# Self attention and its projection in float32r halves held in SBUF, two heads per pass of the array

## The chip, the cores and the metric

The kernel runs on one core of one Trainium2 chip. The metric is the device time of one execution in microseconds (us); of several executions the median is given. Engines are named PE (TensorE matmul), PEld (its weight loads), DVE (VectorE), ACT (ScalarE), POOL (GpSimd) and SP (SyncE, which only begins DMAs here).

## What is computed

Two decoder layers on x of 2 x 1024 tokens by 256. The change touches only the first sublayer, and the way the constants, the tokens and the context matrix reach SBUF ahead of it:

```python
def _L0_attn_ref(x, Wqkv, bqkv, Wout, bout):          # 16 heads of 16
    qkv = jnp.einsum('bsd,hde->bhse', x, Wqkv) + bqkv[None, :, None, :]
    q, k, v = jnp.split(qkv, 3, axis=-1)
    score = jnp.einsum('bhsd,bhtd->bhst', q, k)
    score = jnp.where(causal[None, None], score, -jnp.inf)
    attn = jax.nn.softmax(score / jnp.sqrt(16), axis=-1)
    y = jnp.einsum('bhst,bhtd->bhsd', attn, v)
    return y.transpose(0, 2, 1, 3).reshape(b, s, d) @ Wout + bout
...
x = x + _L0_attn_ref(_layernorm(x), ...)
```

After it come cross attention, a feed-forward part, a recurrence, a second cross attention and a mixture of experts, which the diff leaves alone.

## The kernel before

The program is a row of blocks; at the end of each, all engines meet.

`setup` (L111) loads the tokens and lets POOL make identity and masks; `make_context` (L802) transposes the context. `project_self` (L242) normalises the tokens (`LayerNorm`), transposes them, and forms q and k in float32 (16 sums of two float32 matmuls of 512 tokens, L306; the profile has two records for each float32 matmul), then v (L316). ACT and DVE cut every q and k into three bfloat16 parts (L334 to L366), and SP writes them to DRAM (L276). 32 DMAs (L268) bring the biases for q and k, one for each head.

`SelfAttention(Attention)` (L693, L413) works in 8 units: one batch entry and four heads each. SP brings a unit's q and k from DRAM into a slot (L740, 12 DMAs of 128 KB), three units ahead, laid out so that 96 rows of one matmul hold the six products of parts. Each unit has two phases. In the first, a *piece* is one score matmul of 128 queries by up to 512 keys (L751); where the block lies on the diagonal a mask is added by a second matmul (L754), and DVE takes the row maxima from PSUM (L759). Pieces alternate between two PSUM banks. The maxima are transposed (*turn*, L538), negated, cut into three parts by DVE (L636 to L649) and sent by SP (L504) as three more rows under q. In the second phase a *chunk* (L772, mask L776) gives the scores transposed with the maximum already taken off, ACT takes the exponential (L787), and *weigh* (L796) multiplies four heads' weights by v into one PSUM area, each head in its own 32 columns of the array. ACT copies the sum out (L586), PE transposes it (L568) and DVE divides (L662, L666).

PE carries out all of this in one fixed order, which `order` writes out: unit u's chunks are mixed evenly with unit u + 1's pieces. Every engine is in order, so a wait of PE holds all that stands behind it. The first unit's pieces have no chunks beside them; the last unit's chunks have no pieces.

`project_out` (L830) is the same before and after.

Of the kernel before, what the change touches and what calls it, by code (L numbers as in the profile page):

```python
# [110 lines left out]
def setup(c):  # L111

    nc = c.nc
    x_in, const, cast = c.sig("x_in"), c.sig("const"), c.sig("const_cast")
    with nc.Block() as block:
        @block.sync
        def _(sp):
            for b in range(4):
                sp.dma_start(c.x[:, 4 * b:4 * b + 4, :],
                                      c.arg["x"].rearrange("b (t p) d -> p (b t) d", p=P)[:, 4 * b:4 * b + 4, :]).then_inc(x_in.sem, 16)  # L120
            sp.wait_ge(x_in.sem, x_in.at(64))

        @block.gpsimd
        def _(pool):
            link = Chain(const)
            pool.memset(c.ident[:, :], 0.0).then_inc(link.sem, 1)
            pool.wait_ge(link.sem, link.next())
            pool.affine_select(out=c.ident[:, :], in_=c.ident[:, :], compare_op=ALU.not_equal, fill=1.0,
                                    base=0, pattern=[[-1, P]], channel_multiplier=1).then_inc(link.sem, 1)
            pool.wait_ge(link.sem, link.next())  # L130
            pool.memset(c.maxmask[:, :], 0.0).then_inc(link.sem, 1)
            pool.wait_ge(link.sem, link.next())

            pool.affine_select(out=c.maxmask[:, :], in_=c.maxmask[:, :], compare_op=ALU.is_ge, fill=MASKED,
                                    base=0, pattern=[[-1, P]], channel_multiplier=1).then_inc(link.sem, 1)
            pool.wait_ge(link.sem, link.next())
            pool.memset(c.expmask[:, :], 0.0).then_inc(link.sem, 1)
            pool.wait_ge(link.sem, link.next())

            pool.affine_select(out=c.expmask[:, :], in_=c.expmask[:, :], compare_op=ALU.is_ge, fill=MASKED,  # L140
                                    base=0, pattern=[[1, P]], channel_multiplier=-1).then_inc(link.sem, 1)
            pool.wait_ge(link.sem, link.next())
            pool.iota(c.iota[:, :], [[1, 8]], base=0, channel_multiplier=0,
                           allow_small_or_imprecise_dtypes=True).then_inc(link.sem, 1)
            pool.wait_ge(link.sem, link.next())

        @block.vector
        def _(dve):
            dve.wait_ge(const.sem, const.at(2))
            dve.tensor_copy(c.identb[:, :], c.ident[:, :]).then_inc(cast.sem, 1)  # L150
    for signal, n in ((x_in, 64), (const, 7), (cast, 1)):
        signal.passed(n)


# [78 lines left out]
def head_parts(c, ctx, name):  # L233

    t = {}
    t["full"] = c.sb(ctx, name + "_full", [P, 2, 512], F32)
    t["rest"] = c.sb(ctx, name + "_rest", [P, 2, 512], F32)
    t["part"] = c.sb(ctx, name + "_part", [P, 2, PARTS, N], BF16)
    return t


def project_self(c, v_all, scr_q, scr_k):  # L242

    nc, ps = c.nc, c.ps
    wqkv, bqkv = c.arg["L0_attn_Wqkv"], c.arg["L0_attn_bqkv"]
    with ExitStack() as ctx:
        ln = LayerNorm(c, ctx, "ln0")
        xt = c.sb(ctx, "xt0", [P, KD, N], F32)
        w = c.sb(ctx, "w_qkv", [P, KD, H, 3 * DH], F32)
        w_qk = c.sb(ctx, "w_qk", [P, 2, KD, D], F32)  # L250
        bias = c.sb(ctx, "b_qk", [P, 2, KD], F32)
        bias_v = c.sb(ctx, "b_v", [P, H, DH], F32)
        t = head_parts(c, ctx, "h0")
        w_in, full, high, rest, mid, low, sent, v_set, v_zero = (
            c.sig("w_in"), c.sig("pr_full"), c.sig("pr_high"), c.sig("pr_rest"), c.sig("pr_mid"), c.sig("pr_low"),
            c.sig("pr_sent"), c.sig("pr_v"), c.sig("pr_vzero"))
        mm = c.sig("pr_mm")
        w_set = c.sig("pr_wset")
        blocks = [(i, mb) for i in range(2) for mb in range(KD)]
        NC = N // 512  # L260
        with nc.Block() as block:
            @block.sync
            def _(sp):
                for k in range(KD):
                    sp.dma_start(w[:, k, :, :], wqkv.rearrange("h (k p) e -> k p h e", p=P)[k]).then_inc(w_in.sem, 16)
                for i in range(2):
                    for h in range(H):
                        sp.dma_start(bias[DH * (h % 8):DH * (h % 8) + DH, i, h // 8:h // 8 + 1],  # L268
                                              bqkv[h:h + 1, DH * i:DH * i + DH].rearrange("a b -> b a")).then_inc(w_in.sem, 16)
                sp.dma_start(bias_v[:, :, :], bqkv[:, 2 * DH:3 * DH].partition_broadcast(P)).then_inc(w_in.sem, 16)  # L270
                for n, (i, mb) in enumerate(blocks):

                    sp.wait_ge(mid.sem, mid.at(NC * (n + 1)))
# [75 lines left out]
            def _(dve):  # L349
# [9 lines left out]
                for n in range(len(blocks) * NC):  # L359
# [8 lines left out]
                    if n >= 1:  # L368
                        lows(n - 1)
# [3047 lines left out]
```

## Time and profile before

| what | us |
|---|---|
| median of 3 runs (1902.81 to 1908.55) | 1905.12 |
| the profiled execution | 1912.87 |
| its span, first to last instruction | 1911.2 |
| front blocks, to the last value of v | 0 to 84 |
| memory fills and first loads of the attention, no matmul | 84 to 112 |
| first unit's pieces alone, to its turn | 112 to 144 |
| seven units' pieces beside the chunks of the unit before | 144 to 414.5 |
| the last chunks, no pieces | 414.5 to 455.5 |
| the output projection of the attention | 455.5 to 480.5 |
| all the rest | 480.5 to 1911 |

A busy time counts an instruction from its start to its end; matmuls overlap in the array, so the distance between the starts of two of them tells what one takes in a stream, while the duration of one holds the way through the array as well. [...]

### The profile page before, as it was taken

How to read it: one execution, taken by the hardware profiler on the slowest of the kernel's cores; microseconds unless marked ns; L12 is line 12 of the kernel's file. 1: busy time of each engine (PE TensorE's matmuls, PEld its weight loads, DVE VectorE, ACT ScalarE, POOL GpSimd, SP SyncE). 2: the span in 40 equal slices, each digit the busy share in tenths (PEclk: the TensorE clock that was granted, in tenths of full speed). 3: DMA queues.
4: the chain of work that ended last, by engine and by line, in shares of the span. 5: the costliest groups of instructions: out<-in, count | busy, mean ns of one | idle time of the engine just before them, and what ended most of it. 6: DMA issues, size and time to landing. Idle time of an engine off the chain costs nothing. (4 is left out here: it accounts for less than half of the span.)

```text
span 1911.2 us, 28538 instructions
## 1 busy us (share of the span) xinstructions
PE 1438.0 (75%) x10307; PEld 1073.4 (56%) x10307; DVE 1089.6 (57%) x2450; ACT 898.0 (47%) x2137; POOL 308.2 (16%) x338
## 2 busy tenths in 40 slices
PE   4758889988589999789981453588868059999964
PEld 2413333334379999656760231477755059999953
DVE  3657766741655555455668647456553047777753
ACT  1503555553256666331104775366542057887731
POOL 1200000002223333200001525100010600000034
PEclk8858999998799999979995665799887579999987
DMA  2371322200200000110000000211112256766623
GB/s 68 132 99 20 49 35 35 35 2 9 81 1 2 1 1 2 34 39 1 0 23 9 1 6 14 64 35 34 34 47 88 88 188 219 222 216 217 227 85 103
DMA packets 92688, 122.59 MB, mean 64 GB/s; under 512 B 22221, under 2 KB 74051, under 8 KB 92291
## 3 DMA queue, kind: packets, MB, share of 16 engines
q1 hardware_dynamic: 86675, 105.85, 20.5%
q0 software_dynamic: 4912, 14.42, 2.1%
q8 instruction: 83, 1.36, 0.3%
q10 hardware_dynamic: 960, 0.47, 0.1%
q14 instruction: 58, 0.48, 0.1%
HBM read 88.60 MB, written 24.67 MB: 59 GB/s over the span
## 5 line engine op out<-in xcount | busy, mean ns | idle before, releaser
L759 DVE TENSOR_REDUCE sa_top<-ps 128x1 f32<-128x512 f32 (+3 forms) x384 | 197.2, 553 | 96.3 <-PE ps L751 65.3
L787 ACT ACTIVATE sa_probs<-ps 128x1024 f32<-128x1024 f32 (+4 forms) x192 | 150.8, 811 | 204.1 <-PE ps L772 145.6
L751 PE MATMUL ps<-sa_k,sa_q 96*128 96x512 bf16 (+3 forms) x384 | 125.5, 365 | 55.5 <-DMA sa_k<-scr_k 28.5
L1983 PE MATMUL ps<-me_h,me_w_parts 128*128 128x256 f32 x1104 | 142.0, 289 | 14.5 <-DVE me_w_parts L2058 7.9
L1983 PEld LDWEIGHTS ps<-me_h,me_w_parts 128*128 128x128 f32 x1104 | 136.8, 192 | 18.7 <-issue 15.3
L1997 PE MATMUL ps<-me_w_parts,me_mid 128*128 128x256 f32 x1104 | 136.2, 283 | 6.1 <-DVE me_result L2075 6.1
L1997 PEld LDWEIGHTS ps<-me_w_parts,me_mid 128*128 128x128 f32 x1104 | 132.3, 188 | 10.5 <-issue 10.5
L2735 ACT ACTIVATE cx_p<-ps,cx_top 128x154 f32<-128x154 f32 x256 | 97.2, 389 | 86.4 <-DVE cx_top L2799 86.4
L751 PEld LDWEIGHTS ps<-sa_k,sa_q 96*128 96x128 bf16 x384 | 35.1, 98 | 160.7 <-DVE sa_top L759 89.1
L2058 DVE TENSOR_TENSOR me_w_parts<-me_chunk,me_w_parts 128x1024 fp32r<-128x1024 f32 x92 | 112.8, 1226 | 21.4 <-ACT me_w_parts L2023 18.6
L2045 ACT ACTIVATE me_full<-ps,me_b 128x256 f32<-128x256 f32 x184 | 95.0, 517 | 57.6 <-PE ps L1983 54.5
L2086 DVE TENSOR_TENSOR me_mid<-me_full,me_mid 128x256 fp32r<-128x256 f32 x184 | 76.9, 422 | 65.8 <-ACT me_mid L2047 65.8
L772 PE MATMUL ps<-sa_q,sa_k 99*128 99x512 bf16 (+3 forms) x384 | 108.2, 335 | 7.6 <-ACT sa_probs L787 7.5
L2023 ACT ACTIVATE me_w_parts<-me_chunk 128x1024 fp32r<-128x1024 f32 x92 | 104.6, 1137 | 3.8 <-DMA me_chunk<-in_L_ffn_W_dram 3.8
L3164 ACT ACTIVATE cn_p<-ps,cn_top 128x154 f32<-128x154 f32 x256 | 82.1, 397 | 43.7 <-DVE cn_top L3248 43.5
L2047 ACT ACTIVATE me_mid<-ps,me_b 128x256 fp32r<-128x256 f32 x184 | 96.2, 523 | 0.0
L2597 POOL TENSOR_TENSOR cx_pn<-cx_p,cx_rinv 128x512 f32<-128x512 f32 x64 | 66.8, 1043 | 171.3 <-DVE cx_rinv L2807 171.2
L1058 PE MATMUL ps<-f_w_high,f_hid 128*128 128x512 f32 (+1 forms) x320 | 91.9, 373 | 0.0
L796 PE MATMUL ps<-sa_probs,v_all 128*32 128x512 f32 (+3 forms) x768 | 76.9, 503 | 0.0
L850 POOL TENSOR_TENSOR x<-x,po_b 128x256 f32<-128x256 f32 x16 | 11.0, 727 | 361.8 <-DMA po_w<-in_L_attn_Wout_dram 361.8
L772 PEld LDWEIGHTS ps<-sa_q,sa_k 99*128 99x128 bf16 x384 | 38.0, 100 | 49.5 <-ACT sa_probs L787 16.9
L1957 POOL DMA_DIRECT2D moe_results<-me_result x23 | 16.6, 720 | 301.1 <-DVE me_result L2075 301.1
(397 smaller groups left out, 3530.7 us busy)
## 6 DMA issues: line engine op xcount, KB each, us to landing
me_chunk<-in_L_ffn_W_dram SPq DMA_DIRECT2D x92, 512.0 KB, 5.4
sa_q<-scr_q SPq DMA_DIRECT2D x48, 128.0 KB, 4.8
sa_k<-scr_k SPq DMA_DIRECT2D x48, 128.0 KB, 7.7
moe_rows<-mp_zeros SPq DMA_DIRECT2D x2, 2944.0 KB, 12.7
me_row<-moe_rows SPq DMA_DIRECT2D x23, 256.0 KB, 3.8
moe_results<-me_result POOLq DMA_DIRECT2D x23, 256.0 KB, 3.2
cn_qd<-cn_qh SPq DMA_DIRECT2D x64, 64.0 KB, 2.0
scr_q<-h_part SPq DMA_DIRECT2D x6, 512.0 KB, 3.9
```

Of the source, the lines that this page charges most:

```text
L751: last = pe.matmul(c.ps[:, bank, 0:w], self.q_st[0:96, slot, h, P * sb:P * sb + P], self.k_st[0:96, slot, h, k0:k0 + w], start=True, stop= ...
L759: return dve.tensor_reduce(self.top2[:, k0 // 512, ST * h + sb:ST * h + sb + 1], self.c.ps[:, bank, 0:w], AX.X, ALU.max)
L772: last = pe.matmul(out[:, 0:qw], self.k_st[0:KROWS, slot, h, P * kb:P * kb + P], self.q_st[0:KROWS, slot, h, P * kb + q0:P * kb + q0 + qw] ...
L787: return act.activation(dst, src, ACT.Exp, scale=self.width ** -0.5)
L1058: last = pe.matmul(ps[:, 4 + n % 4, 0:w], hid[:, g % 2, net, m, part, cols], wt[:, m, w0:w0 + w], start=(i == 0), stop=(i == len(terms) - 1))
L1983: last = pe.matmul(ps[:, MID + n % 4, 0:RT], w[:, u % 2, 0, i, DM * k + P * b:DM * k + P * b + P], h[:, u % 2, j, k, :], start=(m == 0), s ...
L1997: last = pe.matmul(ps[:, OUT + n % 2, 0:D], mid[:, u % 2, b, i, P * a:P * a + P], w[:, u % 2, 1, j, D * b:D * b + D], start=(m == 0), stop ...
L2023: act.activation(part(n, 0), chunk[:, n % BUF, :], ACT.Copy).then_inc(w_high.sem, 1)
L2045: act.activation(full[:, n % 4, :], ps[:, MID + n % 4, 0:RT], ACT.Relu, bias=col).then_inc(s_full.sem, 1)
L2047: act.activation(mid[:, u % 2, b, 0, :], ps[:, MID + n % 4, 0:RT], ACT.Relu, bias=col).then_inc(high.sem, 1)
L2058: dve.tensor_tensor(part(n, 1), chunk[:, n % BUF, :], raw(part(n, 0)), ALU.subtract).then_inc(w_low.sem, 1)
L2735: last = act.activation(p[:, h + i, :], ps[:, S_BANK + n % SR, M * i:M * i + M], ACT.Exp, bias=top[:, t % 2, h + i:h + i + 1], accum_out=d ...
```

## The change

`setup`, `make_context` and `project_self` become one block, `front`. Tokens come in four DMAs with a semaphore each, in between other loads. The biases go through a small DRAM tensor and come back in four DMAs. ACT does the scaling of the LayerNorm. Tokens and weights are cut into two float32r halves (high and low), and each product of the projection is three float32r matmuls (high by high, high by low, low by high) in place of one in float32: per group of 512 tokens 4 blocks x 6 matmuls of 512 columns and 4 x 6 of 256. q and k stay in SBUF as two float32r halves (`hi`, `lo`); nothing is written to DRAM. POOL cuts the weights (6 copies, 6 subtractions).

`SelfAttention` is rewritten. A head's scores need 3 x 16 = 48 rows, at rows 0 to 47 for one head and 64 to 111 for another, so that two matmuls (`for a in range(2)`) use different halves of the array. Units are halved into 16 subs by queries (`SUBS`): the lower half of the queries has 8 piece pairs and 8 chunk pairs, the upper half 16 and 16. The number and width of DVE's reductions is unchanged (384), as is that of the exponentials' elements. SP alone begins all copies from `hi` and `lo` to the slots, 24 of 64 KB for each unit. Pieces, turns and outs share a ring of three PSUM banks; a pair waits for both its banks at once. `order` sorts by a timetable in which a sub's chunks begin 5 us after its maxima and then follow one another at ACT's pace. POOL fills 32 rows of two halves of the key tile with ones, 6144 float32 columns each, and SP waits for that. The maxima take two parts in place of three.

```diff
 class SelfAttention:
+    SLOTS = 3
+    MAX_RING = 3
+    EXP_BANK = (3, 5)
+    OUT_BANK = 7
...
+        self.k = sb("k", [P, self.SLOTS, 2, S], F32R)
...
+        for k in range(len(SUBS)):
+            for n, (p, sb, k0, w) in enumerate(self.pieces(k)):
+                items.append((dve, "piece", k, n))
+                dve += 2 * (0.075 + w / 960)
+            items.append((dve, "join", k, 0))
+            items.append((dve + 1.2, "turn", k, 0))
+            dve += 1.0
+            act = max(act, dve + 5.0)
+            for n, (kb, p) in enumerate(self.chunks(k)):
+                items.append((act - 0.9, "chunk", k, n))
+                act += 0.12 + 2 * self.span(k, kb)[1] / 1200
+                if p == 1:
+                    items.append((act + 0.9, "weigh", k, kb))
+            items.append((act + 1.0, "copy", k, 0))
+            items.append((act + 3.0, "out", k, 0))
+            act += 0.6
+            dve += 0.9
...
+        def stage(eng, u, i, dst, done):
+            b, g = UNITS[u]
+            for a in range(2):
+                for j, part in enumerate(((self.hi, self.lo, self.hi), (self.hi, self.hi, self.lo))[i]):
+                    for p in range(2):
+                        r = 64 * (g % 2) + 32 * p + DH * a
+                        to = raw(dst[64 * a + DH * j:64 * a + DH * j + DH, u % self.SLOTS])
+                        src = raw(part[r:r + DH, KD * i + g // 2, S * b:S * b + S])
...
+            def _(sp):
+                for u in range(min(self.SLOTS, len(UNITS))):
+                    if u == 0:
+                        sp.wait_ge(s["made"].sem, s["made"].at(2))
+                    stage(sp, u, 0, self.q, self.q_in[u])
+                    stage(sp, u, 1, self.k, self.k_in[u])
+                for k, (u, half) in enumerate(SUBS):
+                    sp.wait_ge(s["freed"].sem, s["freed"].at(uses["turn", k, 0][0] + 1))
+                    for part, neg in enumerate((self.negh, self.negl)):
+                        for a in range(2):
...
+                    if k % 2 and k >= 3 and (k - 3) // 2 + self.SLOTS < len(UNITS):
+                        v = (k - 3) // 2
+                        sp.wait_ge(s["weighed"].sem, s["weighed"].at(step0[last_of_unit[v] + 1]))
+                        stage(sp, v + self.SLOTS, 0, self.q, self.q_in[v % self.SLOTS])
+                        stage(sp, v + self.SLOTS, 1, self.k, self.k_in[v % self.SLOTS])
...
+            def _(pool):
+                for a in range(2):
+                    pool.memset(self.k[64 * a + 32:64 * a + 64, :, :, :].bitcast(F32), 1.0).then_inc(s["made"].sem, 1)
...
+                    banks = [take(m) for m in uses["piece", k, n]]
...
+                    for a in range(2):
+                        r = slice(64 * a, 64 * a + 3 * DH)
+                        last = pe.matmul(ps[:, banks[a], 0:w], self.q[r, slot, half, p, q0:q0 + P], self.k[r, slot, p, k0:k0 + w],
+                                         start=True, stop=not diagonal)
...
+                    if diagonal:
+                        for a in range(2):
+                            pe.matmul(ps[:, banks[a], w - P:w], c.identb[:, :], c.maxmask[:, :], start=False,
+                                      stop=True).then_inc(s["filled"].sem, 1)
```

## Rows read from the trace of the kernel before

**Rows 1.** Busy time by stretch: stretch, us, then PE, PEld, DVE, ACT, POOL, clock, DMA share, GB/s.

```profile
0.00:84.10 84.10, 54.66 (x168) 32.38 (x168) 43.52 (x110) 31.87 (x57) 7.31 (x17) 0.94 0.35 114
84.10:111.80 27.70, 0.00 (x0) 0.00 (x0) 7.00 (x2) 1.28 (x1) 13.86 (x4) 0.53 0.50 67
111.80:144.40 32.60, 24.81 (x80) 6.77 (x80) 25.35 (x49) 0.00 (x0) 0.00 (x0) 0.50 0.68 89
144.40:414.60 270.20, 242.09 (x1785) 102.16 (x1789) 190.39 (x404) 134.70 (x168) 0.00 (x0) 0.97 0.22 31
414.60:455.50 40.90, 32.47 (x260) 12.44 (x255) 3.54 (x12) 23.53 (x33) 0.00 (x0) 0.92 0.01 2
```

**Rows 2.** The page's costliest groups (line, form, count; busy us, mean ns; idle before, releaser).

```profile
L759 DVE TENSOR_REDUCE sa_top<-ps 128x1 f32<-128x512 f32 (+3 forms) x384 | 197.2, 553 | 96.3 <-PE ps L751 65.3
L787 ACT ACTIVATE sa_probs<-ps 128x1024 f32<-128x1024 f32 (+4 forms) x192 | 150.8, 811 | 204.1 <-PE ps L772 145.6
```

**Rows 3.** Timeline up to the first piece (start us, duration us, engine and instruction, idle before).

```profile
15.21 1.41 DVE L175 BATCH_NORM_STATS2 ln_stats<-x 128x6 f32<-128x256 f32 x4 [0.32 <-PEq L808]
...
32.97 0.42 SPq L270 DMA_DIRECT2D b_v<-in_L_attn_bqkv_dram  x1
...
38.52 30.72 PE L306 MATMUL ps<-xt,w_qk 128*128 128x512 f32 x64 [7.99 <-POOL w_qk L289]
...
43.77 0.34 PEld L306 LDWEIGHTS ps<-xt,w_qk 128*128 128x128 f32 x1 [0.52 <-issue]
...
44.61 0.19 PEld L306 LDWEIGHTS ps<-xt,w_qk 128*128 128x128 f32 x1 [0.50 <-issue]
...
84.11 13.86 POOL L726 MEMSET sa_k<- 32x4096 bf16 x4 [45.69 <-POOLq L261]
...
98.00 2.67 SPq L740 DMA_DIRECT2D sa_q<-scr_q  x6
...
111.85 1.03 PE L751 MATMUL ps<-sa_k,sa_q 96*128 96x512 bf16 x2 [28.49 <-DMA sa_k<-scr_k]
```

**Rows 4.** Groups by form, ACT, DVE and POOL: durations used for `front` and the fills.

```profile
L1328 ACT ACTIVATE bi_y<-bi_y,bi_shift,bi_scale 128x256 f32<-128x256 f32 x48 | 25.3, 608 | 22.6 <-DVE bi_minus L1320 22.6
...
L366 DVE TENSOR_TENSOR h_rest<-h_full,h_part 128x512 f32<-128x512 f32 x16 | 11.1, 693 | 23.6 <-ACT h_part L336 23.6
...
L282 POOL MEMSET v_all<- 128x4096 f32 x1 | 3.5, 3512 | 12.0 <-POOLq L808 12.0
```

**Rows 5.** Timeline of PE in the first cross attention: float32r matmuls of 256 columns.

```profile
600.90 0.28 PE L2681 MATMUL ps<-cx_woh,cx_ol 128*128 128x256 f32 x1
601.02 0.28 PE L2681 MATMUL ps<-cx_wol,cx_oh 128*128 128x256 f32 x1
```

**Rows 6.** Issue time on SP of 64 KB and 128 KB copies (duration ns min/median/max).

```profile
L2972 SPq DMA_DIRECT2D cn_qd<-cn_qh x64: 585/597/1601, 1208.9 to 1377.6; - x64
...
L740 SPq DMA_DIRECT2D sa_q<-scr_q x48: 330/426/583, 98.0 to 342.4; - x48
```

**Rows 7.** The page's DMA issues (KB each, median us to landing): an SBUF to SBUF copy.

```profile
cn_qd<-cn_qh SPq DMA_DIRECT2D x64, 64.0 KB, 2.0
```

**Rows 8.** Timeline of PE around one *weigh*, clock 1.00.

```profile
380.01 0.27 PE L772 MATMUL ps<-sa_q,sa_k 99*128 99x256 bf16 x1
380.12 0.22 PE L776 MATMUL ps<-expmask,identb 128*128 128x128 bf16 x1
380.27 1.06 PE L796 MATMUL ps<-sa_probs,v_all 128*32 128x512 f32 x8
381.27 0.61 PE L751 MATMUL ps<-sa_k,sa_q 96*128 96x512 bf16 x2
```

**Rows 9.** Groups by form: DVE's steps for each unit, and ACT's widest exponential.

```profile
L636 DVE TENSOR_SCALAR sa_neg_rest<-ps 32x128 f32<-32x128 f32 x8 | 2.2, 278 | 3.7 <-PE ps L538 3.7
L666 DVE TENSOR_TENSOR o_tok<-ps,sa_rinv 128x256 f32<-128x256 f32 x16 | 6.8, 424 | 0.6
L787 ACT ACTIVATE sa_probs<-ps 128x1024 f32<-128x1024 f32 x48 | 46.9, 1023 | 89.0 <-PE ps L772 72.6 <-PE ps L796 13.0 <-PE ps L776 3.4
```

More of the change, by code:

```diff
@@ L108, in new_stage @@
         self.signals = {}
[L111 to L152, printed above, removed]
 class LayerNorm:
@@ L230, in done, with front @@
             self.s[k].passed(n)
[L233 to L242, printed above, removed]
+VC = DH + 1
+def front(c, ct, hi, lo, v_all, scratch):
     nc, ps = c.nc, c.ps
     wqkv, bqkv = c.arg["L0_attn_Wqkv"], c.arg["L0_attn_bqkv"]
+    scr_b = scratch("scr_b0", [3, H, DH], F32)
+    G = NT // 4
@@ L246, in project_self @@
     with ExitStack() as ctx:
[L247 to L260, printed above, removed]
+        sb = lambda n, shape, dt=F32: c.sb(ctx, "fr_" + n, shape, dt)
+        raw_ctx = sb("ctx", [MH, 4, DC])
+        w = sb("w", [P, KD, H, 3 * DH])
+        wh, wl = sb("wh", [P, 3, KD, D], F32R), sb("wl", [P, 3, KD, D], F32R)
+        bias, bias_v = sb("b", [P, 2, KD]), sb("bv", [P, H, DH])
+        stats, mv = sb("stats", [P, NT, 6]), sb("mv", [P, NT, 2])
@@ L261, in project_self @@
+        c_turned, c_set, turned, x_high, x_low, filled, high, cleared = (
+            c.sig("f_" + k) for k in ("c_turned", "c_set", "turned", "x_high", "x_low", "filled", "high", "cleared"))
+        NB = 5
+        T_BANK, R_BANK, RING = 0, 4, 4
+        blocks = [(i, m) for i in range(2) for m in range(KD)]
+        PER = len(blocks) + 4
         with nc.Block() as block:
@@ L266, in _ @@
+                sp.dma_start(raw_ctx[:, :, :], c.arg["ctx_768"].rearrange("b (i m) d -> m (b i) d", m=MH)).then_inc(c_in.sem, 16)
+                sp.wait_ge(b_out.sem, b_out.at(16))
                 for i in range(2):
[L267 to L270, printed above, removed]
@@ L271, in _ @@
[L271 to L278 removed]
+                    for m in range(KD):
+                        sp.dma_start(bias[:, i, m:m + 1],
+                                     scr_b[i, 8 * m:8 * m + 8, :].rearrange("h (e a) -> (h e) a", a=1)).then_inc(b_in.sem, 16)
@@ L310, in _ @@
-                for u in range(NT):
-                    if u < 8:
-                        pe.wait_ge(high.sem, high.at(n - 7 + u))
-                    else:
-                        pe.wait_ge(v_set.sem, v_set.at(u - 7))
-                    for k in range(KD):
-                        last = pe.matmul(ps[:, (n + u) % 8, 0:D], xt[:, k, P * u:P * u + P],
-                                         w[:, k, :, 2 * DH:3 * DH], start=(k == 0), stop=(k == KD - 1))
-                    last.then_inc(mm.sem, 1)
```

841 lines of the change are left out of this document (395 added, 446 removed).

## The prediction

> **What bounds the kernel now.** I read the page's costliest groups first, then the busy time by stretch, then the timeline at the borders of the stretches. The change ends where the output projection of the attention begins, at 455.5 us of the span; the 1455.7 us behind that run the same instructions on the same data layout and are taken as unchanged. The sum is made against the profiled execution, 1912.87 us, which lies 7.75 us above the median of the runs shown (1905.12); the difference that I find is taken off the median at the end. A difference under 0.3% (5.7 us) can hardly be told from none here.
>
> The 455.5 us fall in two. Up to the first piece of the attention, at 111.85 us [rows 3], the array is often idle: it works 54.7 of the first 84 us and not at all in the next 27.7 [rows 1]. The projection's first matmul comes at 38.52, since POOL copies the weights only after the last of 35 loads (the one for v's bias is begun at 32.97), and between the projection's end and the first piece stand POOL's fills, 13.86 us, and the loads of the first unit, begun at 98.0 and waited for until 111.85 [rows 3]. From the first piece on, 343.6 us, no engine is full by itself: the first unit's pieces take 32.6 us, then seven units take 270.2, that is 38.6 each, and the last chunks 40.9 [rows 1]. In the middle stretch PE is busy 242.1 of 270.2 us, DVE 190.4, ACT 134.7 [rows 1]. DVE's reductions are the largest group, 197.2 us, and stand idle 96.3 us, most of it for pieces [rows 2]. So PE, in its fixed order, sets the pace, and DVE would be next with 220.1 us: 197.2 [rows 2] and 16 times the small steps of a sub, two like the negation at 0.28, the division at 0.42 [rows 9], and join and reciprocal, which I put at 0.45 together by the same rows: 1.43 x 16 = 22.9.
>
> **Up to the first piece.** The first tokens are begun at the start, as now; I allow 4.8 us for them. Then: statistics 1.41 for four tiles [rows 3] and 0.5 for the small steps after them, about 0.7 for root, reciprocal and shift, four normalisations on ACT at 0.61 [rows 4] (2.4), eight transposes 2.3, the high half about 1.2, the low half 0.7 like the subtraction of 693 ns [rows 4]: 14.0, with the semaphores 14.5 us. The weights are begun before 4 us and cut by about 17 us, and the first product needs a third of that; the biases come in six DMAs instead of 33. Both are hidden by the LayerNorm; if they were 3 us late, all that follows is 3 us late. PE's part is then 4 groups of 24 matmuls of 512 and 24 of 256 columns. A float32r matmul of 256 columns takes 0.12 us in a stream [rows 5]; with 0.23 for 512 that is 8.4 us for each group, 33.6 in all, plus 4.6 for the two transpose groups that stand between them. The clock is low at first: loads came 0.85 us apart until 44.6 and half that afterwards, six us after the first matmul [rows 3]; 3 us for that. DVE has 16 low halves at 0.69, and ACT as many high ones, less than PE in each group. The end is 14.5 + 33.6 + 4.6 + 3.0 + 0.8 for the last values = 56.5 us, against 84.1.
>
> What comes after is not shorter by much. A fill of 4096 elements takes 3.51 us in float32 and 3.47 in bfloat16 (13.86 / 4) [rows 3, 4], so it goes by elements; the new ones have 6144, 5.27 us each, 10.5 for both, and SP waits for both: 67.4. Then 24 copies of 64 KB instead of 12 of 128 KB. Issue takes 0.60 for a copy from SBUF to SBUF and 0.43 for a plain one from DRAM [rows 6]; the copies of q have the form of the former and those of k that of the latter, so I take 0.55, with 0.43 and 0.65 as ends. 24 x 0.55 = 13.2, and 2.0 to land [rows 7]: the first piece at 82.6 instead of 111.85, **29.2 us gained**. The DRAM copies of the parts that fall away lay under PE's v matmuls and give nothing by themselves.
>
> **The SP queue.** Now the maxima's rows go out when they are ready. After the change SP begins three whole units before it looks at the first sub: 72 x 0.55 = 39.6 us, then four row copies at 0.6 (2.4) and 1.9 to land, so the first rows arrive 43.9 us after the first copy was begun, 28.7 after the first piece. PE comes to the first chunk after about 12 us (6.5 for the first sub's reductions, 1.0, and 5 less 0.9 by the timetable). Everything that stands behind it on PE, pieces too, waits 16.7 us; DVE can still empty the ring: **16 lost**. Later SP loads a unit after each of the subs 3, 5, 7, 9 and 11, 13.2 us, and the next sub's rows stand behind it. They arrive 2.4 + 13.2 + 2.4 + 1.9 = 19.9 us after the turn before. After subs 3, 7 and 11 comes a short sub (some 11 us) and PE wants them after 15: 4.9 late, of which DVE hides 1.5: **10 lost** in three places (none if PE is late itself, 15 at most).
>
> **The piece and chunk work.** ACT's exponentials come in bursts. A two-head exponential of 1024 elements takes 0.98 in a stream (46.9 / 48) [rows 9]; an upper sub has 16, eight of them narrower, 13.6 us; a lower one 5.5. In 13.6 us DVE wants 12 pairs of pieces (24 pairs in 27.5 us), in 5.5 about 5. What PE needs for this:
> - [...] I take 0.24 for every width.
> - A diagonal pair has two masks more, each 0.055 (from L776 to L772, 0.06 [rows 8]): 0.11. They use all 128 rows, so the array changes between half height and full height and back.
> - A weigh: 0.85 of columns; entering it costs 0.10 (the mask before it started 0.15 earlier and needs 0.055) and leaving it 0.15 (1.00 from start to start) [rows 8]. Wide 1.10, the narrower ones 0.78 on average.
>
> No row has a change of height. Its bounds are 0, as between L772 and L776, which follow each other without a gap, and 0.10 to 0.15, as around the weigh [rows 8]. Nearest is the weigh, another change of how the array is cut; but there four heads' loads must come first as well, so I take **0.05**. Counting the written order, there are 461 such changes and 178 around weighs.
>
> [...]
>
> Upper burst: 8 x 0.24 + 8 x (0.24 + 0.11 + 0.10) + 4 x 1.10 + 4 x 0.78 + 12 piece pairs, one third plain and two thirds diagonal, at 0.38 (4.6) = 17.6 us against 13.6; lower: 8 x 0.45 + 4 x 0.78 + 5 x 0.38 = 8.6 against 5.5. So PE is late by 4.0 + 3.1, say 7.3 with the transposes, in each of seven units: **51 us** on top of DVE's 220. Between bursts PE has pieces only, and before the change that was done at a clock of 0.50 (112 to 144 us) [rows 1]; the timetable has four gaps of near 10 us. Each costs up to 3 us until the clock is back, as in the projection; PE's lateness shortens them: **8 us** (0 to 30). After the last maxima there remain the end of sub 14's exponentials and sub 15's: **20 us**, against 40.9 now.
>
> Sum from the first piece: 220 + 16 + 10 + 51 + 8 + 20 = 325 us against 343.6, **18.6 gained**. Together with 29.2 it is 47.8: the profiled execution would take 1865, the median 1905.1 - 47.8 = **1857 us**.
>
> **The rivals.**
> 1. *The change of height is free*, or PE's order leaves slack enough. Then a diagonal pair takes 0.35, the bursts are late by 2.4 and 2.1, 32 us in all: 1838. With no lateness of PE at all it is 1806. For it speaks that masks follow without any gap now [rows 8]; against it, that the present unit takes 38.6 us where PE's streams sum to about 31, so that in-order waiting costs something always.
> 2. *It is as dear as around the weigh*, 0.10 to 0.15: 70 to 90 us late instead of 51, 1876 to 1896.
> 3. *The two heads don't run side by side*, since the change doesn't do what it says. Then a pair of 512 columns takes 0.45; 84 us late, 1890. No row has two matmuls in different rows; that the weigh runs four heads in the time of one (0.85 for what would be 3.4) [rows 8] speaks against it for columns. [...]
> 4. *Slower: one after another and dear changes together.* PE's upper burst then takes 24.9 against 13.6 and the lower 12.2 against 5.5: 18 us a unit, 126 in all, and 4 more in the tail. That is 404 from the first piece: 1936. It decides as soon as PE is late by 14 us a unit.
> 5. *Slower: SP falls behind.* Should a copy hold SP for 1.0 us (the worst of the present ones took 1.6 [rows 6]), the first unit lands 10.8 later, the first stall grows by 21, and after each load the next rows are 16 us late after short subs and 3.5 after long ones: 54 instead of 10. 76 us more: 1933. It decides from 0.8 us a copy. The median of 0.60 and the landing in 2.0 [rows 6, 7] speak against it.
>
> **How the numbers follow.** My forecast (1843 to 1872) has 0.48; rival 1, 0.22; rival 2, 0.12; rival 3, 0.05; rival 4, 0.06; rival 5, 0.07. Faster by over 0.3% means under 1899.4: the forecast, rival 1, 0.10 of rival 2 and 0.01 of rival 3: 0.81. Within 0.3%: 0.02 and 0.04 of rivals 2 and 3: 0.06. Slower: rivals 4 and 5: 0.13. The range reaches from rival 1 without lateness, 1805, to just past rivals 2 and 3, 1910, and leaves out rivals 4 and 5 and the little below 1805.
>
> **What would show it.** The first matmul of `front`'s products near 14 us and the fills from 56 to 67; the first piece near 83; then a stall of PE of some 16 us at the first chunk, waiting for a DMA. Two matmuls of a pair starting within 0.1 us of each other; the distance from the second to the mask, less 0.21, is the price of the change of height. Reductions must still be busy 197 us, idle much less than 96. If ACT's idle time in bursts is small and DVE is busy over nine tenths, rival 1 holds; if pairs start 0.21 apart, rival 3. The prediction fails if the clock stays at 0.50 beyond the first unit, which I price at 30 us at most.

## The result, and the profile after

The changed kernel is slower: 1988.96 us median of 4 runs (1979.21 to 1995.48) beside 1904.49 for the kernel before (1902.81 to 1908.55), a ratio of 1.0436 with a 95% interval of 1.0384 to 1.0488. The profiled execution has a span of 1993.5 us, 82.3 more than before.

Busy time by stretch (columns as in [rows 1]): the front end, the gap before the first piece, the first pieces and chunks, the middle up to the last piece, the last chunks.

```profile
0.00:61.50 61.50, 43.41 (x232) 36.97 (x232) 32.06 (x86) 25.18 (x45) 8.84 (x24) 0.97 0.23 54
61.50:89.40 27.90, 0.00 (x1) 0.03 (x1) 0.00 (x1) 1.28 (x1) 10.42 (x2) 0.58 0.35 58
89.40:133.00 43.60, 21.31 (x89) 9.20 (x89) 15.48 (x35) 4.26 (x5) 0.00 (x0) 0.50 0.43 71
133.00:520.80 387.80, 345.75 (x1877) 135.20 (x1873) 200.61 (x423) 140.93 (x181) 0.00 (x0) 0.64 0.13 22
520.80:545.00 24.20, 20.07 (x169) 7.89 (x167) 1.92 (x6) 15.55 (x22) 0.00 (x0) 0.98 0.01 3
```

The first piece comes at 89.4 in place of 111.85, 22.4 us earlier [rows 3]. The part behind the attention takes 1450 us in place of 1456. All of the loss lies between: from the first piece to the last output of the attention (at 543.3, before 455.2) it is 453.9 us in place of 343.4. PE is again the busiest, 345.75 of 387.80 us in the middle, but the granted clock there is 0.64 where it was 0.97 [rows 1]. Every record of the granted clock in this trace is 1.00 or 0.50, 32 of each, so 0.64 means that the array stood at 0.50 for some seven tenths of the stretch.

The page's groups, to be held against [rows 2]: the reductions and the exponentials are as long as before, and their idle time is what grew, for DVE from 96.3 to 215.5 us.

```profile
L675 DVE TENSOR_REDUCE sa_top<-ps 128x1 f32<-128x512 f32 (+3 forms) x384 | 196.2, 553 | 215.5 <-PE ps L592 145.5
L653 ACT ACTIVATE sa_probs<-ps 128x1024 f32<-128x1024 f32 (+1 forms) x192 | 152.4, 810 | 298.0 <-PE ps L617 173.8
L586 PE MATMUL ps<-sa_k,sa_q 48*128 48x512 f32 (+3 forms) x384 | 114.6, 586 | 69.9 <-DVE sa_top L675 40.8
```

Timeline of the changed kernel at the start of the attention: the fills, the first copies, the first pair, and the wait at the first chunk.

```profile
61.79 10.47 POOL L565 MEMSET sa_k<- 32x6144 f32 x2 [46.30 <-POOLq L220]
...
72.29 1.32 SPq L535 DMA_DIRECT2D sa_q<-qk_high  x2
73.66 1.23 SPq L535 DMA_DIRECT2D sa_q<-qk_low  x2
74.93 2.50 SPq L535 DMA_DIRECT2D sa_q<-qk_high  x4
...
89.40 0.47 PE L586 MATMUL ps<-sa_k,sa_q 48*128 48x128 f32 x2 [28.36 <-DMA sa_k<-qk_low]
...
122.58 0.80 PE L613 MATMUL ps<-sa_q,sa_k 50*128 50x512 f32 x2 [14.62 <-DMA sa_q<-sa_negl]
```

And two places in PE's timeline at full clock, 1.00. A pair stands in one line ("x2"); both heads start within 0.04 us of each other.

```profile
454.61 0.50 PE L586 MATMUL ps<-sa_k,sa_q 48*128 48x512 f32 x2
454.94 0.33 PE L613 MATMUL ps<-sa_q,sa_k 50*128 50x384 f32 x2
...
524.28 0.50 PE L613 MATMUL ps<-sa_q,sa_k 50*128 50x512 f32 x2
524.71 0.29 PE L617 MATMUL ps<-expmask,identb 128*128 128x128 bf16 x2
524.93 0.50 PE L613 MATMUL ps<-sa_q,sa_k 50*128 50x512 f32 x2
```

So the heads do run side by side: a pair of 512 columns is followed by the next pair 0.33 us later, where one after another would need 0.43 for the columns alone: at full clock a matmul of 512 columns is followed by the next 0.21 us later (e5, at 282.63). 0.33 is 0.21 for the columns and 0.12 more. A float32r weight load that is not hidden would fit, as an estimate of mine (the loads of these pairs last 0.18 us each from 440 to 460, those of the bfloat16 masks 0.10, and float32r matmuls of 256 columns stood 0.12 apart [rows 5]); no run tests it. With masks it is 0.43 from the pair to them and 0.22 from them to the next pair: 0.10 more going in, and 0.11 more than the masks' own columns (0.107 at that rate) going out. A diagonal pair of 512 columns costs 0.65 where the prediction had 0.45 for every width.

The clock is not low everywhere in this kernel. From 440 to 460 us, with pieces and chunks, and in the last chunks from 520.8 us on, it is 1.00 and 0.98, with the same pairs of 48 and 50 rows a head.

### The profile page after: what moved, and what is told of

Same layout as the page of the kernel before. It is cut to its first block and busy times, and to the rows that moved or that the text cites. A ratio compares the mean times of both kernels' runs of the same rounds, so it can differ in the third digit from the quotient of the medians.

```text
span 1993.5 us, 28893 instructions
## 1 busy us (share of the span) xinstructions
PE 1522.3 (76%) x10379; PEld 1112.4 (56%) x10379; DVE 1069.6 (54%) x2424; ACT 892.9 (45%) x2133; POOL 305.8 (15%) x343
## 5 line engine op out<-in xcount | busy, mean ns | idle before, releaser
L675 DVE TENSOR_REDUCE sa_top<-ps 128x1 f32<-128x512 f32 (+3 forms) x384 | 196.2, 553 | 215.5 <-PE ps L592 145.5
L653 ACT ACTIVATE sa_probs<-ps 128x1024 f32<-128x1024 f32 (+1 forms) x192 | 152.4, 810 | 298.0 <-PE ps L617 173.8
L586 PE MATMUL ps<-sa_k,sa_q 48*128 48x512 f32 (+3 forms) x384 | 114.6, 586 | 69.9 <-DVE sa_top L675 40.8
L1908 PEld LDWEIGHTS ps<-me_w_parts,me_mid 128*128 128x128 f32 x1104 | 132.6, 188 | 10.5 <-issue 10.5
L586 PEld LDWEIGHTS ps<-sa_k,sa_q 48*128 48x128 f32 x384 | 52.6, 254 | 132.6 <-DVE sa_top L675 83.3
L613 PE MATMUL ps<-sa_q,sa_k 50*128 50x512 f32 (+3 forms) x384 | 106.8, 560 | 15.8 <-DMA sa_q<-sa_negl 14.6
L628 PE MATMUL ps<-sa_probs,v_all 128*17 128x512 f32 (+3 forms) x768 | 112.2, 674 | 0.0
L613 PEld LDWEIGHTS ps<-sa_q,sa_k 50*128 50x128 f32 x384 | 48.5, 251 | 97.5 <-issue 51.3
L969 PEld LDWEIGHTS ps<-f_w_high,f_hid 128*128 128x128 f32 x320 | 58.2, 189 | 11.7 <-issue 1.4
```

Source lines behind the costliest of these rows:

```text
L586: last = pe.matmul(ps[:, banks[a], 0:w], self.q[r, slot, half, p, q0:q0 + P], self.k[r, slot, p, k0:k0 + w], start=True, stop=not diagonal)
L613: last = pe.matmul(ps[:, bank + a, 0:w], self.k[r, slot, p, P * kb:P * kb + P], self.q[r, slot, half, p, q0:q0 + w], start=True, stop=not ...
L628: last = pe.matmul(ps[VW * h:VW * h + VC, self.OUT_BANK, q0:HALF], self.v_all[:, ST * b + kb, HPU * g + h, :], self.probs[:, (step0[k] + k ...
L653: act.activation(self.probs[:, (g // 2) % self.PROBS, p, :, 0:w], ps[:, bank:bank + 2, 0:w], ACT.Exp, scale=DH ** -0.5).then_inc(s["exped" ...
L675: dve.tensor_reduce(self.top2[:, k % 2, k0 // 512, col:col + 1], ps[:, m % self.MAX_RING, 0:w], AX.X, ALU.max).then_inc(s["freed"].sem, 1)
L969: last = pe.matmul(ps[:, 4 + n % 4, 0:w], hid[:, g % 2, net, m, part, cols], wt[:, m, w0:w0 + w], start=(i == 0), stop=(i == len(terms) - 1))
```

## The experiments

Two causes stood open. Theory C: the granted clock is the loss, and short bursts with gaps between them keep it low. Theory S: the changes of height are the loss. The second experiment brought theory R: the clock is the loss, and it follows the rows that the matmuls use. Differences of a few us between kernels that were not timed side by side are not read; "attention" is the stretch from the first piece to the last output in the profiled execution.

| kernel | ratio to before (95%) | median us | attention us | clock in it |
|---|---|---|---|---|
| before | 1 | 1904.5 | 343 | 0.92 |
| changed | 1.0436 (1.0384 to 1.0488) | 1989.0 | 454 | 0.65 |
| e1 masks at half height | 1.0196 (1.0141 to 1.0252) | 1947.1 | 406 | 0.67 |
| e2 one after another | 1.1348 (1.1326 to 1.1370) | 2165.6 | 623 | 0.51 |
| e3 chunks twice | 1.0342 (1.0316 to 1.0367) | 1971.8 | 432 | 0.78 |
| e4 chunks spread | 1.0375 (1.0349 to 1.0401) | 1976.4 | 431 | 0.68 |
| e5 before, 48 rows | 1.0435 (1.0399 to 1.0471) | 1988.4 | 428 | 0.65 |
| e6 full height, zeros | 1.0308 (1.0274 to 1.0342) | 1962.1 | 424 | 0.82 |
| e7 e6, masks 64 rows | 1.0529 (1.0482 to 1.0576) | 2006.3 | 465 | 0.79 |
| e8 e6, no maxima's masks | 1.0165 (1.0137 to 1.0192) | 1937.6 | 403 | 0.82 |
| e9 before, 66 rows | 1.0174 (1.0112 to 1.0236) | 1935.4 | 380 | 0.79 |
| e10 before, no maxima's masks | 0.9962 (0.9943 to 0.9982) | 1894.4 | 335 | 0.93 |
| e11 combined | 0.9888 (0.9857 to 0.9920) | 1881.2 | 353 | 0.88 |
| e12 e11, later copies | 0.9905 (0.9881 to 0.9929) | 1878.2 | 359 | 0.87 |

**e1: masks at half height.**

```diff
-  pe.matmul(ps[:, banks[a], w - P:w], c.identb[:, :], c.maxmask[:, :], start=False,
+  r = slice(64 * a, 64 * a + 64)
+  pe.matmul(ps[:, banks[a], w - P:w], c.identb[r, :], c.maxmask[r, :], start=False,
```

(and the same for expmask)

> The changed kernel with each mask matmul on the same 64 rows as the head whose scores it masks (rows 0 to 63 for the first head, 64 to 127 for the second), so that no mask changes the height of the rows used. Left out: the other half of each mask, so half of the masked scores are counted. It takes away 256 of the 461 changes of height in the attention, and keeps every column. Theory S (the changes of height are the loss: 0.22 us in and 0.11 out at full clock, 0.30 and 0.11 at half, with the gaps that follow): 80 to 110 us less than the changed kernel, 1880 to 1910. Theory C (the granted clock is the loss: 0.64 in the attention where the kernel before had 0.97, because two heads beside each other leave the array with gaps between short bursts): the clock stays below 0.75 in the attention and the time is 1945 to 1975.

42 us less than the changed kernel, with the clock still at 0.67. The time, 1947, lies at the lower edge of what theory C allowed and far from the 1880 to 1910 of theory S. Yet the attention is 48 us shorter, so the changes beside the masks are a real part of the loss, less than half of the 110 us. Counted in the written order, all changes of height fall from 569 to 217, so 352 are gone, not the 256 of the expectation (256 is the number of groups of masks). The masks also use fewer rows here, which the run does not keep apart.

**e2: one after another.**

```diff
-  r = slice(64 * a, 64 * a + 3 * DH)
+  r = slice(0, 3 * DH)
```

> The changed kernel with both heads of a pair read from rows 0 to 47 (0 to 49 in the chunks), so that the two matmuls run one after another. Left out: the odd heads' own queries and keys (the even head's stand in their place). Instructions, waits and changes of height stay as they are; the columns that TensorE streams for scores double. Theory C: the array is in use for longer without a gap, the granted clock goes to 0.9 or more in the attention, and the time is 1900 to 1990, no slower than the changed kernel. Theory S: the clock has no part in it, the pairs' doubled columns add 0.21 us at full clock to each 512-column pair and 0.4 at half, and the time is 2030 to 2080.

Busy time of e2 from the first piece to the last output:

```profile
90.40:713.50 623.10, 576.77 (x2128) 265.40 (x2128) 218.67 (x464) 163.37 (x208) 0.00 (x0) 0.51 0.11 19
```

It is 177 us slower than the changed kernel, and both theories miss it, C most of all: PE is busy for 0.93 of the time and the clock is at its lower level almost throughout. Idle time is not what keeps the clock down here. The most visible difference from the middle of the kernel before [rows 1], at 0.97 and no busier, is that a score matmul uses 48 or 50 rows of the array and not 96 or 99; float32r and the changes of height differ too, and e5 leaves those two out or nearly so.

The last chunks show the same without any piece. They take 24.2 us at a clock of 0.98 in the changed kernel (the last line of its stretches above), where the two heads' rows are in use together. In e2, one head after another, PE has no gaps to speak of and the clock is 0.50:

```profile
668.00:713.50 45.50, 43.93 (x182) 16.64 (x181) 3.39 (x9) 17.89 (x24) 0.00 (x0) 0.50 0.00 1
```

**e3: the chunks' matmuls twice.**

```diff
-  for a in range(2):
+  for i in range(4):
+      a = i % 2
```

> The changed kernel with the two score matmuls of every chunk begun twice into the same bank, so that TensorE streams more columns without a new wait and without a new change of height. The result is the same. Theory C: the fuller bursts raise the granted clock above 0.7 in the attention, which pays for them: 1950 to 1990. Theory S: the 320 extra pairs cost their own time at the clock as it is, 0.2 to 0.45 us each beside a TensorE that is the bound: 2020 to 2080.

384 matmuls more (192 pairs; the expectation says 320), and 17 us less: the clock rises to 0.78, and the added columns pay for themselves. The intervals of the two ratios do not touch, though barely. That fits C and R and is against S as the whole cause.

**e4: chunks spread.**

```diff
-  act += 0.12 + 2 * self.span(k, kb)[1] / 1200
+  act += 1.4 * (0.12 + 2 * self.span(k, kb)[1] / 1200)
```

> The changed kernel with another timetable: the pace at which the order of work places the chunks is 1.4 times slower, so that chunks are spread over the whole of a sub's maxima instead of being finished in its first part, after which TensorE waits for VectorE between pieces. No instruction is added or taken away. Theory C: fewer stretches in which TensorE has only pieces, a clock above 0.7 in the attention, 30 to 60 us less, 1930 to 1960. Theory S: more changes between pieces and chunks are no change of height, so the number of those stays and the time is within 15 us of the changed kernel, 1975 to 2005.

13 us less by the medians, 23 in the profiled attention, so under the 30 to 60 that C wanted; the intervals of the two ratios overlap, and the clock hardly moves, 0.68. The order of work is not the main thing.

**e5: the kernel before with 48 rows.**

```diff
-  last = pe.matmul(c.ps[:, bank, 0:w], self.q_st[0:96, slot, h, P * sb:P * sb + P],
-                   self.k_st[0:96, slot, h, k0:k0 + w], start=True, stop=not diagonal)
+  last = pe.matmul(c.ps[:, bank, 0:w], self.q_st[0:48, slot, h, P * sb:P * sb + P],
+                   self.k_st[0:48, slot, h, k0:k0 + w], start=True, stop=not diagonal)
```

(chunks likewise; masks over rows 0 to 63)

> The kernel before, with its score matmuls over the first 48 of their 96 or 99 rows and its mask matmuls over 64 of 128. Left out: the lower parts of the queries and keys, the subtracted maximum, and half of each mask. The bytes moved, the instructions, the waits and the columns streamed are those of the kernel before, and no change of height is put beside a mask; only the rows that each matmul uses fall. Theory R, formed on e2, where TensorE was busy for 534 of 560 us with score matmuls of 48 and 50 rows and the granted clock stayed at 0.51: the clock falls with the rows in use, not with the gaps; here the attention, at 0.97 before, falls to below 0.7, and the time rises by 90 us or more, above 1995. Theory C (columns and gaps alone set the clock): the clock stays above 0.9 and the time is within 15 us of the kernel before, 1890 to 1920.

**e9: the same with 66 rows**, for pieces, chunks and masks.

> The kernel before, with its score matmuls and its masks over the first 66 rows in place of 96, 99 and 128. Left out: part of the lower halves of queries and keys, the subtracted maximum and half of each mask. It is e5 with 66 rows for 48 and 64: nothing else differs from it, except that no matmul of the attention then stands at another height than its weighs (in e5 the changes around the weighs were left). If e5's 83 us are the clock and follow the rows (theory R), the granted clock here lies between e5's 0.64 and the 0.94 to 0.97 of the kernel before, about 0.75, and the time is 1940 to 1980. If e5's loss was the changes of height around the weighs, the clock is above 0.9 and the time 1900 to 1920.

The middle of the attention in e5 and in e9; the line of the kernel before is the fourth of [rows 1].

```profile
144.40:500.00 355.60, 339.51 (x1800) 133.34 (x1799) 190.85 (x405) 137.87 (x170) 0.00 (x0) 0.64 0.17 23
```

```profile
144.40:440.00 295.60, 269.42 (x1751) 108.31 (x1750) 187.18 (x393) 132.67 (x165) 0.00 (x0) 0.84 0.20 28
```

This is the decisive pair. Same bytes, same order, same columns, no float32r, no heads side by side: with 96 to 99 rows (128 in the masks) the clock in the middle is 0.97, with 66 it is 0.84, with 48 (64 in the masks) it is 0.64, and the attention takes 343, 380 and 428 us. Theory R stands in direction, and both sizes were a little overstated: e5 came out at 1988, not above 1995, and e9 at 1935, not 1940 to 1980, with a clock above the expected 0.75. e9's three runs spread from 1922 to 1945, and the profile is of the slowest, so its 380 us may be some 10 too many. e5 still has changes of height around 64 weighs and 24 groups of transposes; at the 0.22 us that e7 shows for in and out they are 19 of its 85 us. e9 has none of them and still loses clock.

The rows set no fixed level. e9 stands at 1.00 from 220 to 260 us and at 0.50 from 350 to 380, with PE busy for 29.86 of these 30 us. What starts and ends such a stretch was not found.

**e6: full height with zeros.** A pair's keys lie one above the other, each head has its own query tile, and there are two slots for a unit in place of three:

```diff
-  self.q = sb("q", [P, self.SLOTS, 2, 2, HALF], F32R)
+  self.q = sb("q", [P, self.SLOTS, 2, 2, 2, HALF], F32R)
...
-  r = slice(64 * a, 64 * a + 3 * DH)
-  last = pe.matmul(ps[:, banks[a], 0:w], self.q[r, slot, half, p, q0:q0 + P],
+  r = slice(0, 6 * DH)
+  last = pe.matmul(ps[:, banks[a], 0:w], self.q[r, slot, a, half, p, q0:q0 + P],
```

> The changed kernel with its two heads no longer beside each other: a pair's keys lie one above the other in rows 0 to 95, each head has its own query tile with zeros in the rows of the other head, and each score matmul uses all 96 rows (98 with the rows of the maximum), so it gives one head alone. Two slots for a unit in place of three, the next unit's copies begun half a unit earlier; the fills in pieces, one slot ahead of the first copies. The result is the same. TensorE streams twice the changed kernel's score columns, and no matmul changes the height. Theory R: the granted clock is back above 0.9 in the attention; with the columns of the kernel before and the first piece at about 82 us, the time is 1840 to 1890. Theory S (changes of height alone, the clock apart): 2 x 0.213 us in place of 0.25 for a pair at full clock, less 0.33 for each of the 288 diagonal pairs, about 50 us better than the changed kernel, 1920 to 1950. If neither holds (columns and gaps alone), it is 1990 or more.

Faster than the changed kernel by 27 us with twice its score columns, but at 1962 it met none of the expectations: R's 1840 to 1890 was far off, S's 1920 to 1950 nearer. Some of its stretches:

```profile
180.00:190.00 10.00, 9.06 (x40) 4.38 (x38) 3.51 (x10) 2.05 (x2) 0.00 (x0) 0.50 0.01 2
...
200.00:210.00 10.00, 9.67 (x77) 5.80 (x73) 5.94 (x14) 5.33 (x7) 0.00 (x0) 1.00 0.01 2
...
270.00:280.00 10.00, 7.53 (x28) 3.67 (x26) 3.31 (x8) 5.93 (x6) 0.00 (x0) 0.72 0.63 105
280.00:290.00 10.00, 7.28 (x30) 4.35 (x30) 2.49 (x8) 1.20 (x2) 0.00 (x0) 0.62 0.05 10
```

Away from the gaps the clock is full in places, 1.00 from 200 to 210. Where the next unit's copies are late (the DMA share of 0.63 at 270) PE falls idle, busy for 7.53 and 7.28 us of ten, and the clock falls with it to 0.72 and 0.62, and the work behind such a gap starts at 0.50, as from 180 to 190 (PE was busy for 0.41 us of 175 to 180). So gaps seem to matter too, once the rows are there. The slot that was given up is one reason for them: SP waits 35.7 us in all for weighs to free a slot before it copies, which it never does in the changed kernel, and PE waits 8.3 us for keys.

**e7: e6 with masks over 64 rows.**

```diff
-  pe.matmul(ps[:, banks[a], w - P:w], c.identb[:, :], c.maxmask[:, :], start=False,
+  pe.matmul(ps[:, banks[a], w - P:w], c.identb[0:64, :], c.maxmask[0:64, :], start=False,
```

(and the same for expmask)

> The kernel of e6 with its mask matmuls over 64 of their 128 rows, so that the 288 groups of masks change the height in and out again, as in the changed kernel, while nearly all columns stream over 96 rows. Left out: half of each mask. If the price of a change that the trace of the changed kernel shows at full clock holds here (0.22 in, 0.11 out), it is 60 to 95 us slower than e6. If the changes cost what the prediction took (0.05), 15 to 30 us slower. If what looked like their price was the low clock alone, within 10 us of e6.

PE's timeline at full clock, first e6, then e7, at the same kind of pair:

```profile
254.94 0.59 PE L615 MATMUL ps<-sa_q,sa_k 98*128 98x384 f32 x2
255.38 0.29 PE L619 MATMUL ps<-expmask,identb 128*128 128x128 bf16 x2
255.48 0.71 PE L588 MATMUL ps<-sa_k,sa_q 96*128 96x512 f32 x2
```

```profile
322.89 0.61 PE L615 MATMUL ps<-sa_q,sa_k 98*128 98x384 f32 x2
323.44 0.28 PE L619 MATMUL ps<-expmask,identb 64*128 64x128 bf16 x2
323.65 0.73 PE L588 MATMUL ps<-sa_k,sa_q 96*128 96x512 f32 x2
```

To the masks 0.44 against 0.55, from them 0.10 against 0.21: a change of height costs 0.11 us each way. There are 256 groups of masks (128 at pieces, 128 at chunks; the expectations of e6 and e7 have 288), and at 0.22 they are 56 us. The attention grew by 41; part of the price may lie beside waits. This agrees roughly with e1, where 352 changes at 0.11 are 39 us and 48 were found. The expected 60 to 95 was too much: the 0.22 "in" had been read from a place where the pair itself already took 0.12 more than its columns, changes or not.

e7 also has a reading on the rows in the program of the changed kernel. e2 and e7 both compute one head after another with the same columns, and both change height at every group of masks. With 48 and 50 rows (e2) the clock is 0.51 and the attention 623 us; with 96 and 98 rows, half of them zeros for each head (e7), it is 0.79 and 465 us. e2's further changes at weighs and transposes can't make up 158 us: even all of its 569 changes, at 0.11 us, are 63, and e7 has 512 itself. So rows that hold zeros count. But after a gap (PE busy for 2.42 us of 185 to 190) e7 stays at 0.50 for long, with PE busy for 39.50 of 40 us:

```profile
190.00:230.00 40.00, 39.50 (x151) 17.57 (x144) 10.87 (x25) 11.84 (x15) 0.00 (x0) 0.50 0.00 1
```

**e8 and e10: without the masks of the maxima.**

```diff
-  diagonal = k0 + w == (sb + 1) * P
+  diagonal = False
```

> The kernel of e6 without the 256 masks of the maxima: a row's maximum is taken over the whole diagonal block, above what the softmax needs, and the result is the same within rounding. Theory R with TensorE as the bound: 256 x 0.06 to 0.12 us less than e6, 15 to 30 us, 1815 to 1870. If VectorE's reduces or the copies are the bound by then, no more than 5 us less.

> The kernel before without the 256 masks of the maxima; the result is the same within rounding. It is the control for e8 and e11. The masks' 128 columns are 0.053 us each at full clock and stand 0.11 apart at half clock: 14 to 28 us less where TensorE is the bound, 1875 to 1895. If the bound was VectorE, within 5 us of the kernel before; if the missing full-height masks lower the granted clock (theory R carried on), the gain is lost in it, 1895 to 1915.

25 us from e6, as much as expected, though at 1938 not the time expected, which had built on a faster e6. In the kernel before it is only 7 by the ratio (8 in the attention), half of the least gain expected, though the clock holds at 0.93. Why it is not more there was not looked into.

**e11: combined.** The diff in its main lines:

```diff
+  QSUBS = 4
-  self.q = sb("q", [P, self.SLOTS, 2, 2, HALF], F32R)
+  self.q = sb("q", [P, self.QSUBS, 2, 2, HALF], F32R)
...
+  for i in range(self.QSUBS):
+      pool.memset(self.q[:, i].bitcast(F32), 0.0).then_inc(s["made"].sem, 1)
...
-  act += 0.12 + 2 * self.span(k, kb)[1] / 1200
+  act += 1.37 * (0.12 + 2 * self.span(k, kb)[1] / 1200)
```

> All that the runs point to, in one kernel with the same result: e8 (full height with zeros, no masks of the maxima), three slots of keys in place of two and query slots of half a unit, so that no copy waits for a unit's end; the first unit's key copies begun by ScalarE beside SyncE's query copies, later key copies by GpSimd; the fills in single slots; and the pace of e4, 1.37, that leaves no stretch with pieces only. Theory R with the gaps of e8 as the rest of its loss (clock 0.84 there, with stretches of 10 us at half clock behind each gap): the clock is 0.95 or more from the second unit on, the first piece comes at 76 to 80 us, the attention lasts 310 to 330 us, and the time is 1845 to 1880. If rows that hold zeros do not count for the clock, it stays near 0.85 without the gaps too, and the time is 1900 to 1930.

It beats both kernels, 1.1% under the one before (interval 0.8 to 1.4), though just beside the expected range. Leaving out the masks of the maxima gives the kernel before 0.4% of that too (e10), so the rest is worth 0.7%. It comes from the earlier first piece, at 85.8: the attention itself takes 353 us at 0.88, not 330 at 0.95, and longer than e10's 335. The copies at the start of e11, SP's and ACT's:

```profile
68.94 3.87 SPq L536 DMA_DIRECT2D sa_q<-qk_high  x4
72.85 2.52 SPq L536 DMA_DIRECT2D sa_q<-qk_low  x2
75.41 8.65 SPq L536 DMA_DIRECT2D sa_q<-qk_high  x4
```

```profile
66.69 2.56 ACTq L536 DMA_DIRECT2D sa_k<-qk_high  x4
69.27 1.65 ACTq L536 DMA_DIRECT2D sa_k<-qk_low  x2
70.95 6.06 ACTq L536 DMA_DIRECT2D sa_k<-qk_high  x4
```

Four issues took 8.65 us on SP (32 KB each) and 6.06 on ACT (64 KB) where SP alone needed 2.50 for four of 64 KB (changed kernel, at 74.93). GpSimd copied at the same time, twelve of 64 KB begun from 71.39 to 77.40. Whether the three queues hold each other up is what e12 asks.

**e12: the later copies wait.**

```diff
+  if k:
+      sp.wait_ge(k_sig(0).sem, k_sig(0).at(k_count(0)))
   sp.wait_ge(s["made"].sem, s["made"].at(k + 1))
   stage_q(sp, k)
```

(ACT and GpSimd wait likewise)

> The kernel of e11 with one edit: the copies that are not for the first sub (its second query half, the second unit's keys, the third unit's keys) wait until the first sub's have landed, the third unit's until its maxima are done. In e11 three queues copied at once from 66.2 us on, the transfer engines were busy for 0.91 to 0.99 of the stretch 70 to 82, four issues took 8.65 us in place of 2.5, and the first piece came at 85.8 where 76 to 80 was expected. If that crowding is the cause, the twelve query and twelve key copies take 8 us side by side, the first piece comes at 75 to 78, and the time is 7 to 11 us less than e11, 1869 to 1875. If two queues alone crowd each other as much, the first piece stays above 82 and the time is within 3 us of e11.

Half right. The first piece comes at 78.5, 7.3 us earlier, so the crowding was the cause. Two queues still crowd each other, but less: the longest four issues took 3.87 us. But the last output comes only 2 us earlier, and the ratio can't be told from e11's, where 7 to 11 us were expected. Where the other 5 us went stays open.

## Why the prediction was wrong

It said 1857 and faster; it is 1989 and slower, outside the range. Step by step:

- **Front end and first piece: right, too optimistic by 6.8 us.** The front end ended at 61.5 where 56.5 was predicted, the fills took 10.47 (10.5), and a copy's issue took 0.62 (2.50 for four) where 0.55 was taken. 22.4 us were gained, not 29.2.
- **SP's queue: nearly right at first, in part by luck, and nothing later.** The wait at the first chunk is 14.62 us (16). Two errors cancel in it: the rows let PE go on 33.2 us after the first piece, not 28.7, and PE came to the chunk after 18.6 us, not 12. The 10 us behind later units did not show: no other wait of PE on a DMA stands in the chain of its waits, since PE itself was late.
- **Side by side: right.** Rival 3 falls. But 0.24 for a pair of any width was too little, and no row or run shows it; the changed kernel's timeline has 0.33 at 512 columns and 0.27 at 384 (from 454.94 to the masks at 455.21), 0.11 to 0.12 over the columns. That this is a weight load was not tested.
- **Change of height: 0.05 predicted, 0.11 measured**, the lower end of rival 2's price. By the prediction's own burst sum, with 0.33 and 0.65 for the pairs, an upper burst takes 8 x 0.33 + 8 x 0.65 + 4 x 1.10 + 4 x 0.78 + 12 x 0.54 = 21.8 in place of 17.6 and a lower one 11.0 in place of 8.6: 46 us more over seven units at full clock, and that is a ceiling, since narrower pairs take less. That alone would have given at most 1903: no loss. The two runs that take the changes out or put them in (e1 and e7) give 48 and 41, at clocks below full.
- **The clock: 8 us predicted, 30 at most; this is the step that failed.** From the attention's 454 us, DVE's 220, the wait of 14.6, the 97 (51 + 46) and a tail of 22 leave some 100 us, or more as the 46 is a ceiling. The prediction asked only whether PE had gaps and priced them between bursts. It took the clock of 0.97 [rows 1] as given for a busy array, and never asked what the halved rows would do to it; what the runs showed is a middle stretch at 0.64 with PE busy for 345.75 of 387.80 us. e5 shows the effect of rows without float32r and without heads side by side: half the rows in the kernel before, 85 us, of which some 19 may be its own changes of height. That the changed kernel loses its clock by the same cause is argued, not isolated: there two heads of 48 rows are in use together, for half as long. More columns side by side (e3, 0.78) and full-height matmuls (e6, 0.82) both bring clock back; more columns one head after another do not (e2, 0.51). The sentence "The prediction fails if the clock stays at 0.50 beyond the first unit" named the symptom and put it at 30 us, without a mechanism.

That the array was kept busy did not bring the full clock: in e2 it was busy for 576.77 of 623.10 us and stayed at 0.51. At an equal clock the number of rows made no difference to a matmul's time: in e5 a matmul of 512 columns over 48 rows was followed 0.21 us later at the full clock (at 282.63), and in the kernel before two of them over 96 rows took 0.44 (381.27 to 381.71). At 0.50 a matmul of 256 columns took as long (0.21 in e5, at 302.12), and 0.50 is where few rows mostly stood (0.64 in the middle of e5 and of the changed kernel). A change from 96 or 98 rows to 64 and back costs 0.11 us each way (e6 and e7).

How the 110 us divide between clock and changes is not settled to better than some 20 us: each change is also a short gap (0.11 us, e7), and at a granted clock of 0.50 PE's matmuls take longer (256 columns 0.21 us in e5, at 302.12, where they took 0.11 at 1.00 [rows 8]). Shown are the parts alone: 41 to 48 us for the changes beside masks (e7, e1), and in the kernel before up to 85 (66 without its own changes) for the rows (e5).

## What to carry to other kernels

A busy array is no promise of a full clock: in e2 it was busy for 0.93 of the attention, at 0.51. Where a change halves the rows that matmuls use, read the granted clock of the stretch, and price the stretch at half clock as a rival of its own, with the array busy (the middle of e5: busy for 339.51 of 355.60 us at 0.64). Halving the rows and running two heads side by side was worth less here than using 96 rows, half of them zeros (1989.0 us against 1962.1 in e6). Before splitting work by height, count the changes in the written order and take for each the 0.11 us that e6 and e7 show between 96 or 98 rows and 64; and take a price from a place in the stream where nothing else is late.

## What the runs showed of the hardware

- The granted clock fell with the rows of the score and mask matmuls while PE stayed busy (for 0.90, 0.91 and 0.95 of the time): 0.97, 0.84 and 0.64 in the middle of the attention for 96 to 99, 66 and 48 rows in the same program (before, e9, e5). One head after another in float32r it was 0.51 over 48 and 50 rows (e2) and 0.79 over 96 and 98, half of them zeros (e7).
- The rows alone do not fix it. PE was busy for 39.50 of 40 us at 0.50 over 96 and 98 rows (e7, 190 to 230), and stood at 0.98 over two times 50 rows side by side (the changed kernel's last chunks). Why a stretch stays at one level stays open.
- More columns can make a kernel faster: e3 has 384 matmuls more and takes 17 us less, with the clock in the attention at 0.78 and not 0.65.
- A change between matmuls over 96 or 98 rows and over 64 costs 0.11 us each way at a granted clock of 1.00: from a pair of 384 columns to its masks 0.55 us and from them 0.21 in e7, where e6, with masks over 128 rows, has 0.44 and 0.10.
- Small copies begun on three queues at once slow each other's issue: 0.62 us each of 64 KB on one queue (changed kernel), 1.5 each of 64 KB and 2.2 each of 32 KB with three (e11, from 70.95 and 75.41).
